# A gated state-space layer on one core: GpSimd weighs tiles in pairs, the state between chunks lies on 128 rows

## What is computed

```python
xr, gate = jnp.split(x @ W_in.T, 2, axis=-1)
xr = xr + t_emb[:, None, :]
xc = silu(conv4(xr) + b_conv)                      # 4 taps in time, per channel
xn = layernorm(xc) * ln_g + ln_b
Bm, Cm, dt = jnp.split(xn @ W_xproj.T, 3, axis=-1) # 16 each
dt = jnp.tanh(dt @ W_dt.T + b_dt) * 0.01
Ad = 1.0 - dt * jnp.tanh(A_log)
Bd = Bm * jnp.minimum(norm(xn), 1.0)
def step(h, inputs):                               # h: 16 x 1024 per batch
    h = jnp.clip(h * ad[:, :, None] + bd[:, :, None] * xt[:, None, :], -10.0, 10.0)
    return h, jnp.einsum('bd,bdh->bh', ct, h)
y = ys + D * xn
return x + (y * silu(gate)) @ W_out.T
```

## Time and profile before

| | |
|---|---|
| three runs | 2098.36, 2100.95, 2104.25 us |
| profiled execution | 2097.88 us, its span 2095.8 us |
| mean granted TensorE clock | 0.976 |
| PE matmul busy | 1936.1 us (92%) |
| DVE busy | 1641.5 us (78%) |
| ACT busy | 1439.5 us (69%) |
| POOL busy | 1801.3 us (86%) |
| HBM read / written | 59.96 MB / 9.18 MB |

### The profile page before, as it was taken

The page is one execution under the profiler, slowest core; times in us unless marked ns, Lnnn a source line. Parts: engine busy times, 40 slices in busy tenths (PEclk is TensorE's granted clock), DMA queues, the critical chain, the costliest instruction groups (busy, mean ns, idle before and its releaser), DMA issues.

```text
span 2095.8 us, 46902 instructions
## 1 busy us (share of the span) xinstructions
PE 1936.1 (92%) x16784; PEld 1466.0 (70%) x16784; DVE 1641.5 (78%) x2075; ACT 1439.5 (69%) x3494; POOL 1801.3 (86%) x1444
## 2 busy tenths in 40 slices
PE   5589999999999999999999999999999999999988
PEld 5467777777777777777677777777777777777765
DVE  3377887888877887878887888887888877888786
ACT  4677667777667777767777767677766777766753
POOL 1389988889988989898889998898998888998887
PEclk8699999999999999999999999999999999999999
DMA  5221222121222122222222222222122212222210
GB/s 174 56 61 43 62 46 61 55 66 47 58 46 61 55 66 51 55 45 63 58 61 54 54 54 55 57 59 61 48 62 46 61 55 61 48 61 47 56 50 16
DMA packets 83016, 120.16 MB, mean 57 GB/s; under 512 B 22352, under 2 KB 51408, under 8 KB 78112
## 3 DMA queue, kind: packets, MB, share of 16 engines
q1 hardware_dynamic: 82784, 117.17, 21.5%
HBM read 59.96 MB, written 9.18 MB: 33 GB/s over the span
## 4 chain that ended last, share of the span: by engine, by line
PE 64%; issue 11%; ACT 11%; DVE 10%; SPq 2%; POOL 1%; DMA 1%; DVEq 0%; ACTq 0%; POOLq 0%
PE ps_y L574 13%; PE ps_job L492 8%; PE ps_fill L547 7%; PE ps_job L455 7%; PE ps_fill L538 7%; PE ps_job L468 5%; PE ps_job L450 4%; DVE ks L984 3%; PE ps_y L554 3%; PE ps_y L560 3%; PE ps_job L462 3%; DVE h L931 2%; PE ps_job L478 2%; ACT xh L668 2%; ACT low L778 2%
## 5 line engine op out<-in xcount | busy, mean ns | idle before, releaser
L1082 POOL TENSOR_TENSOR prod<-ks,crep 128x512 f32<-128x512 f32 x1024 | 1289.2, 1279 | 187.8 <-PE ps_y L574 175.7
L984 DVE TENSOR_TENSOR_SCAN ks<-low,ps_fill 128x512 f32<-128x512 f32 x1024 | 1216.9, 1208 | 266.9 <-PE ps_fill L547 257.4
L778 ACT COPY low<-ps_fill 128x512 f32<-128x512 f32 x1024 | 590.1, 580 | 489.0 <-PE ps_fill L538 485.9
L574 PE MATMUL ps_y<-c_sb,prod 128*128 128x128 f32 x4096 | 613.5, 275 | 2.9 <-POOL prod L1082 1.4
L574 PEld LDWEIGHTS ps_y<-c_sb,prod 128*128 128x128 f32 x4096 | 464.3, 142 | 81.5 <-issue 45.0
L538 PEld LDWEIGHTS ps_fill<-ts,xs 128*128 128x128 f16 x4096 | 317.1, 99 | 172.3 <-issue 11.9
L538 PE MATMUL ps_fill<-ts,xs 128*128 128x128 f16 x4096 | 399.2, 220 | 11.7 <-DMA xs<-h 7.2
L547 PE MATMUL ps_fill<-spans,pick 128*128 128x512 f16 x1024 | 392.2, 383 | 6.8 <-ACT low L778 6.6
L450 PE MATMUL ps_job<-x,w_in 128*128 128x128 f16 x3072 | 226.8, 228 | 46.1 <-ACT xr L730 37.3
L737 ACT ACTIVATE tap<-xr,cols_sb 128x128 f32<-128x128 f32 x768 | 251.4, 391 | 16.3 <-PE ps_job L468 16.2
L450 PEld LDWEIGHTS ps_job<-x,w_in 128*128 128x128 f16 x3072 | 197.4, 103 | 59.6 <-issue 58.3
(11 more groups left out here) (119 smaller groups left out, 2164.7 us busy)
## 6 DMA issues: line engine op xcount, KB each, us to landing
crep<-c_dram SPq DMA_DIRECT2D x32, 1024.0 KB, 4.8
xs<-xh SPq DMA_DIRECT2D x256, 64.0 KB, 2.7
xs<-xl SPq DMA_DIRECT2D x224, 64.0 KB, 2.0
xf<-in_xT SPq DMA_DIRECT2D x32, 256.0 KB, 2.8
res<-in_x SPq DMA_DIRECT2D x32, 256.0 KB, 2.7
out_dram<-res SPq DMA_DIRECT2D x32, 256.0 KB, 2.1
ts<-tth SPq DMA_DIRECT2D x128, 32.0 KB
ts<-tth SPq DMA_DIRECT2D x128, 31.0 KB
```

What stands on the lines that cost most here:

```text
L574: last = mm(ps_y[:, cut], prod[:, s % HOLD, e, :], ident, start=False, stop=(u % 4 == 3 and q == 3 and e == QN - 1), is_transpose=True)
L778: copy(low[:, (TILES * k + s) % RING], ps_fill[:, (TILES * k + s) % RING]).then_inc(sem["low_copied"], 1)
L984: nc.vector.tensor_tensor_scan(ks[:, u % 2, QN * q:QN * (q + 1)].rearrange("d n t -> d (n t)"), low[:, g % RING], ps_fill[:, g % RING], 0. ...
L1082: tt(prod[:, i % HOLD], ks[:, u % 2, part], crep[:, p, part], ALU.mult).then_inc(sem["weighed"], 1)
```

## The change

GpSimd multiplies two tiles in one instruction (128 x 1024) at every odd tile, into two of eight `prod` buffers, and PE transposes five tiles behind in place of four. The state between the chunks is kept as 128 rows (state, channel block) x 128 channels: one transpose for `kend`, one DVE instruction for `h1`, and in place of ACT's two "h0" steps a small matmul "bd" that spreads B and decay of the first time from 16 rows to 128, and four DVE instructions of 128 x 128 or less. x of the first time goes through DRAM (`x0_dram`) to `x0`, and `lend` is copied by a DMA to `lend128`. Some jobs and takes move by one or two points. The core of the diff:

```diff
-LAG = 4
-HOLD = 4
+LAG = 5
+HOLD = 8
-        JOBS = [(3, 2, "z", 0, 1, 1, 1), (3, 4, "gate", 0, 0, 2, 0), (6, 1, "hend", 0, -1, 2, 1),
...
+        JOBS = [(3, 2, "z", 0, 1, 1, 1), (3, 4, "gate", 0, 0, 2, 0), (6, 1, "hend", 0, -1, 1, 1),
...
-        GATED_AT = (39, 7)
+        GATED_AT = (41, 9)
...
-                    sp.dma_start(x0, xn[0:1, pn].rearrange("o (n d) -> o n d", n=1).broadcast_to([1, NS, DI])).then_inc(sem[f"x0_in{pn}"], 16)
+                    since(sp, "x0_in", 16 * j)
+                    sp.dma_start(x0_dram, xn[0:1, pn]).then_inc(sem["x0_out"], 16)
...
+                    sp.wait_ge(sem["x0_out"], 16 * (j + 1))
+                    since(sp, "bd_taken", j)
+                    sp.dma_start(x0[:], x0_dram.broadcast_to([NS, DI])).then_inc(sem["x0_in"], 16)
...
+                    sp.wait_ge(sem["lend_set"], 2 * j + 2)
+                    if exists(k, -1):
+                        sp.wait_ge(sem["hend_taken"], k)
+                    sp.dma_start(lend128[:, pn], lend[:]).then_inc(sem[f"lend_in{pn}"], 16)
...
-                    for e in range(4):
-                        last = tr(ps[0:NS, e * P:(e + 1) * P], kend[:, q, 4 * i + e, :], ident)
+                    last = tr(ps[:, 0:P], kend[:, q].rearrange("d n e -> d (n e)"), ident)
+                elif name == "bd":
+                    last = mm(ps[:, 0:2], spread, bd[:], start=True, stop=True)
...
+                    copy(bd[:, 0:1], bank("zT")[0:NS, 0:1]).then_inc(sem["bd0_set"], 1)
...
-                for i in at("h0", 1):
-                    j, q = k + 1, 1 - p
-                    act.wait_ge(sem[f"x0_in{q}"], 16 * pair(k, p, 1))
-                    act.wait_ge(sem["zT_high"], j + 1)
-                    act.wait_ge(sem["zT_taken"], j + 1)
-                    since(act, "h0_taken", 2 * j + i)
-                    act_fn(bank("h0", i)[0:NS], x0[:, i * BANK:(i + 1) * BANK], ACT.Identity, scale=zT[:, 0, 0:1]
-                           ).then_inc(sem["h0_ready"], 1)
...
-                if point == 41 and exists(k, 1):
-                    act.wait_ge(sem["h0_taken"], 2 * (k + 2))
+                if point == 25 and exists(k, 1):
+                    act.wait_ge(sem["bd_taken"], k + 2)
...
+                if point == TAKE["bd", 0] and exists(k, 1):
+                    u = bank("bd")[:, P:2 * P]
+                    dve.wait_ge(sem["bd_ready"], j + 1)
+                    dve.wait_ge(sem["x0_in"], 16 * (j + 1))
+                    nc.vector.tensor_copy(bd128[:], bank("bd")[:, 0:2]).then_inc(sem["bd_copied"], 1)
+                    dve.wait_ge(sem["bd_copied"], j + 1)
+                    tsc(u, x0[:], bd128[:, 0:1], None, ALU.mult).then_inc(sem["u0_set"], 1)
...
+                        stt(u, h1[:], bd128[:, 1:2], u, ALU.mult, ALU.add).then_inc(sem["u1_set"], 1)
+                        dve.wait_ge(sem["u1_set"], j + 1 - BATCH)
+                    tsc(h1[:], u, CLIP, -CLIP, ALU.min, ALU.max).then_inc(sem["bd_taken"], 1)
...
+                if i % 2 == 0:
+                    return
+                part = slice((q - 1) * QN, (q + 1) * QN)
                 pool.wait_ge(sem["scanned"], g + 1)
                 since(pool, "flipped", g - HOLD + 1)
-                tt(prod[:, i % HOLD], ks[:, u % 2, part], crep[:, p, part], ALU.mult).then_inc(sem["weighed"], 1)
+                h = (g - 1) % HOLD
+                tt(prod[:, h:h + 2].rearrange("d h n t -> d (h n) t"), ks[:, u % 2, part], crep[:, p, part], ALU.mult
+                   ).then_inc(sem["weighed"], 2)
```

More of the change, by code:

```diff
@@ L152, in build @@
         ttl = sb("ttl", [P, NS, SUB], H)
[L154 to L155 removed]
+        h1 = sb("h1", [P, P])
+        x0 = sb("x0", [P, P])
+        lend = sb("lend", [NS, DI])
+        lend128 = sb("lend128", [P, 2, P])
         spans = sb("spans", [P, 2, NS * P], H)
@@ L413, in _ @@
             for c in range(DB):
-                last = mm(ps_fill[:, 2, c * NS:(c + 1) * NS], h1[:, c * P:(c + 1) * P], small[:, 0:NS],
+                last = mm(ps_fill[:, 2, c * NS:(c + 1) * NS], lend[:, c * P:(c + 1) * P], small[:, 0:NS],
                           start=True, stop=True)
@@ L430, in job @@
                 _, parts, name, i, off, per, bank = JOBS[m]
-                if not exists(k, off) or name == "h0":
+                if not exists(k, off):
                     return
@@ L573, in flip @@
                 for e in range(QN):
-                    last = mm(ps_y[:, cut], prod[:, s % HOLD, e, :], ident, start=False,
+                    last = mm(ps_y[:, cut], prod[:, (TILES * k + s) % HOLD, e, :], ident, start=False,
                               stop=(u % 4 == 3 and q == 3 and e == QN - 1), is_transpose=True)
@@ L709, in side @@
                     copy(p_end[:, 1 - p:2 - p], pf[:, 1, P - 1:P]).then_inc(sem["p_kept"], 1)
-                if point == 22 and exists(k, 1):
+                if point == 23 and exists(k, 1):
                     act.wait_ge(sem["recip"], k + 2)
@@ L754, in side @@
                     copy(ch[:, half], bank("carry", i)).then_inc(sem["carry16"], 1)
-                    since(act, "hend_taken", 2 * k)
-                    copy(lend[:, 1 - p, half], bank("carry", i)[0:NS]).then_inc(sem["lend_set"], 1)
+                    if exists(k, 0):
+                        act.wait_ge(sem[f"lend_in{p}"], 16 * pair(k, p, 0))
+                    copy(lend[:, half], bank("carry", i)[0:NS]).then_inc(sem["lend_set"], 1)
                 if point == 27 and exists(k, 1):
@@ L771, in ends @@
                 act.wait_ge(sem["scanned"], TILES * k + NQ * (u + 1))
-                since(act, "hend_ready", 2 * (k - 1))
-                copy(kend[:, p, u, :], ks[:, u % 2, :, P - 1]).then_inc(sem["kend_done"], 1)
+                since(act, "hend_ready", k - 1)
+                copy(kend[:, p, :, u], ks[:, u % 2, :, P - 1]).then_inc(sem["kend_done"], 1)
             def body(k, p):
@@ L880, in side @@
                         ).then_inc(sem["z_taken"], 1)
[L881 to L887, removed]
+                if point == TAKE["hend", 0] and exists(k, -1):
+                    dve.wait_ge(sem["hend_ready"], k)
+                    dve.wait_ge(sem[f"lend_in{1 - p}"], 16 * pair(k, p, -1))
                     if exists(k, 0):
@@ L890, in side @@
                         dve.wait_ge(sem["h1_low"], k + 1)
-                    stt(h1[:, half], lend[:, (k - 1) % 2, half], -1.0,
-                        bank("hend", i)[0:NS], ALU.mult, ALU.add).then_inc(sem["hend_taken"], 1)
+                    stt(h1[:], lend128[:, 1 - p], -1.0, bank("hend")[:, 0:P], ALU.mult, ALU.add
+                        ).then_inc(sem["hend_taken"], 1)
                 for i in range(2):
@@ L909, in side @@
                                                  ALU.mult, ALU.add).then_inc(sem["scan_p"], 1)
[L910 to L917, removed]
-                    stt(bank("h0", i)[0:NS], h1[:, half], first_decay[:], bank("h0", i)[0:NS], ALU.mult, ALU.add
-                        ).then_inc(sem["h0_sum"], 1)
-                for i in range(2):
-                    if point != TAKE["h0", i] + 2 or not exists(k, 1):
-                        continue
-                    half = slice(i * BANK, (i + 1) * BANK)
+                if point == TAKE["bd", 0] and exists(k, 1):
[5 more added lines that the diff above has]
+                    tsc(u, x0[:], bd128[:, 0:1], None, ALU.mult).then_inc(sem["u0_set"], 1)
+                    dve.wait_ge(sem["u0_set"], j + 1)
                     if first_chunk(j):
-                        dve.wait_ge(sem["h0_ready"], 2 * j + i + 1)
                         since(dve, "h1_high", j)
@@ L935, in side @@
                     nc.vector.reciprocal(pf[:, 0], pf[:, 1]).then_inc(sem["recip"], 1)
-                if point == 20 and exists(k, 1):
+                if point == 19 and exists(k, 1):
                     dve.wait_ge(sem["recip"], j + 1)
@@ L1125 @@
     c_dram = nc.dram_tensor("c_dram", (1, NS * P), mybir.dt.float32, kind="Internal").ap()
-    build(nc, aps, out, scratch, r_dram, c_dram)
+    x0_dram = nc.dram_tensor("x0_dram", (1, DI), mybir.dt.float32, kind="Internal").ap()
+    build(nc, aps, out, scratch, r_dram, c_dram, x0_dram)
     r = run_bass_kernel_spmd(nc, [ins], core_ids=[0])
```

56 lines of the change are left out of this document (27 added, 29 removed), and 3 rows, old and new, of the table JOBS.

## The result

The changed kernel took 2084.59 us (median of 4 runs, 2081.55 to 2085.64), the kernel before on the same chip 2099.65 us. The ratio is 0.9922, with a 95% interval of 0.9903 to 0.9942: the gain is real, but it is 15 us (0.8%) and not 90. The time lies above the range of 1975 to 2065.

The account below looks back on a forecast made before the run. PE's work and its standstills were taken to bound the kernel. Terms -2.63 - 0.51 - 0.7 + 0.5 + 0.4 gave -2.9 us a step, over 30 steps rounded to 90: 2097.9 - 90 = 2008 us, range 1975 to 2065.

Parts of the forecast that it names:

- What bounds the kernel: Whole kernel: a step's length is PE's work plus the places where PE stands still, mainly at "xr" and "nb".
- The clock: PE behind the two waits: no more falls of 1.62 us in about one step in three, -0.51 on the mean.
- the rival: PE's clock falls once a step in a stretch of mostly transposes, 49 us back, 2057 us; chance 0.04.
- "hend" and the gate: PE: eight transposes become one, plus "bd", about -0.7; `xn` later at the gate, +0.5, bounds 0 and +1.1.
- SP's queue and the smaller runs of the state's copies: DMA of the state: 3.1 us of room covers the added `lend` copy; 0 taken, bounds 0 and +1.5.
- ACT's backlog: ACT's taps, copies and carries become the next late thing: +0.4 us a step, bounds 0 and +1.5.
- The pair products: POOL saves 3.1 us a step, worth nothing by itself since POOL waits for PE; cost only through later `xn`.
- short step: The kind of step without a clock fall, 61.96 us before, where the next took 63.58.
- the wait moves: Half or more of the gain lost to `x0`, SP's queue or, third, ACT's backlog: 2056 us; chance 0.20.
- nothing moves: New state chain as late as the old, all 2.63 us stay, later gate eats the 0.7: 2098 us; chance 0.07.
- the 2.63 us: PE's waits in tiles 12 and 13, 1.37 and 1.26 us a step: both should go, bounds 0 to -2.63.

Follow-up runs that it names:

- run 7: run 6 with the fourth tap at point 37 in place of 36: 1998.05 us, ratio 0.9514.
- run 6: Changed kernel with `bc` and `pf` each reading one operand from PSUM and the `row_b` sum right behind the `row_g` product: 2013.16 us, ratio 0.9589.
- run 3: Changed kernel with `bc` reading B from PSUM, not SBUF, and "bd" three points later; pairs stay: 2025.45 us, ratio 0.9653.
- run 2: Kernel before with pair products alone, two more `prod` buffers, some points two later, `row_g` for `row_d`: 2071.56 us, ratio 0.9869.
- run 4: Changed kernel with the `row_b` sum right behind the product with `row_g`, no pair between them: 2086.83 us, ratio 0.9947.
- run 10: Kernel before with the buffers and later points of run 2 and `row_g` for `row_d`, but single products: 2155.06 us, ratio 1.0265.
- run 9: run 7 with single products of 128x512 in place of pairs: 1997.75 us, ratio 0.9515.

## Why the prediction was wrong, step by step

**What bounds the kernel: right.** PE's program and its waits set the step. Both large waits left with the "h0" chain. Against the earlier trace rows "nb" now starts without one.

**The clock, -0.51: right.** No step of the changed kernel is of the long kind; four are longer by 0.35 us. The granted clock was 1.00 from 150 to 2060 us, and in a step that I went through in windows of 1 us throughout, the stretch of transposes included, where the rival had it fall. What the pause has to meet for the clock to fall stays open: it stood ahead of every step of the kernel before, and the clock fell in nine.

**"hend" and the gate, -0.7 and +0.5: right in sum, "bd" mis-sized.** The small matmul "bd" takes 0.31 us of PE (1047.30 to the next start at 1047.61), where at most 0.11 had been put. The stretch from `xc` to z gives -0.29. The gate wait is 1.0 us against 0.3, so +0.7 and inside the bounds, and what "hend" saves there is then 1.0 in place of 0.77.

**SP's queue and the smaller runs of the state's copies, 0: right.** PE waits for `xs` three times in all, 7.6 us in the whole execution, against 7.2 us in two waits before. The two copies of the state, with runs of 256 B in place of 2 KB, land a median 3.1 us behind their issue, as before.

**ACT's backlog, +0.4: inside its bounds.** Once the failed step below is out of the way, the wait for `xl` that is left costs 0.59 us (run 7 against run 6), and one tap moved by a point takes it away. The delay is of the kind that I had put there: four activations of a tap stand ahead of ACT's copy of the second carry half, DVE's take of this half (`xl`) follows that, and "out" needs the bank.

**The pair products, "worth nothing by itself": this step failed.** It looked for who waits for POOL's results, found nobody, and took a longer POOL instruction for harmless. It did not look for who stands still while POOL runs. `bc` took 2404 ns where 412 were enough. DVE took "nb" 3.12 us behind its start (1054.24 to 1057.36) where it is 1.02 in run 3 (1026.83 to 1027.85), and the step lost 1.9 us (62.15 against 60.25 in run 3) of the 2.6 that were missing in its first stretch. Of these 1.9 some 1.2 stand in named waits of PE (0.40 + 0.15 + 0.20 + 0.93, against 0.48 that is left in run 3); for the others the trace names no wait.

| first stretch, z to `xc` | us | second, `xc` to z | us |
|---|---|---|---|
| before | 43.02 | before | 18.93 |
| forecast | 40.9 | forecast | 18.7 |
| changed | 43.52 | changed | 18.64 |
| `bc` freed (run 3) | 41.60 | run 3 | 18.65 |
| all edits (run 7) | 41.01 | run 7 | 18.28 |

Without the failed step the forecast would have been near, but not right in every term. Its short step was 61.96 - 2.4 = 59.6, and run 3 measures 60.25 (2025 us, inside the range of 1975 to 2065). Of the 0.65 us between them 0.2 are in "bd" and 0.2 in the tap (0.59 for 0.4); the rest stays open. That run 7 comes out under 2008 is no proof of the sum, since two further edits took away waits that were part of it.

The range of the rival "the wait moves", 2040 to 2090, holds the result, but none of its three causes was the one: ACT was late, as in its third, but because DVE took "nb" late. In size "nothing moves" (2098) was nearer than its 2056, and its mechanism was wrong, since the 2.63 us at "nb" and "xr" did go.

The trace of before held only a faint sign. `bc` took 628 ns there, and only runs 2 and 3 show that 0.39 to 0.41 us is its own length. With a pair in the place of a single product these 0.2 us became 2.

The Trainium skill (SBUF — State Buffer, "Who interferes with whom") states this: "A DVE instruction with two SBUF inputs contends with a GpSimd instruction that reads SBUF". The trace agrees, with 2404 ns beside a pair, 1334 beside a single product and 412 with one operand in PSUM. By that rule the prediction should have had a term for each such DVE instruction, by these traces up to one pair's 2.36 us. It was not drawn on.

What stays open: where exactly `bc` and `pf` meet POOL depends on the phase of the two engines, and I found no way to forecast it. Runs 2, 4 and 10 show it differing from run to run of edits that mean something else. What would take away the gate wait that is left in run 9 (21.1 us in all) wasn't tried.

## What to carry to other kernels

A longer instruction on GpSimd is not free because nobody waits for its result: list the DVE instructions with both operands in SBUF, and price each at up to one running GpSimd instruction (here `bc` at 2.4 us beside a pair of 2.36). If one of two operands can be read from PSUM where it already lies, read it there; here that was worth 59 us, four times what the whole change had given. And where two edits come in one change, compare stretches between jobs that both kernels share: it showed at once which terms had come true.

## What the runs showed of the hardware that was not expected

- A 16x256 product on DVE took 412 ns with one operand in PSUM, and with both in SBUF 1334 and 2404 ns beside products of 1.28 and 2.36 us on GpSimd, and 0.39 us where none ran (run 2). A scan of 16x127 took 408 ns, and with both in SBUF 924 to 1361 ns; in the kernel before, where it mostly began 0.11 us ahead of the end of GpSimd's instruction, it took 0.41.
- All 349 that were held ended 0.27 to 0.28 us behind the end of GpSimd's running instruction, whatever its length.
- Scans of 128x512 with one operand in PSUM took 1208 ns beside the same pairs.
- 0.57 us more of waiting ahead of a stretch of matmuls (2.9 in place of 2.3 us in two named waits) went with a fall of the clock in each of 23 steps in a row, where before it fell in nine of 31, and with 2155 us in place of 2099.
